# Latent attention loop: the pieces of the next heads made 512 queries at a time, their second set exchanged by four transfers

## The reference, cut to what matters

```
c_q = h @ w_down_q.T
c_kv = h @ w_down_kv.T
q = (c_q @ w_up_q.T).reshape(b, s, H, DH).transpose(0, 2, 1, 3)
k = (c_kv @ w_up_k.T).reshape(b, s, H, DH).transpose(0, 2, 1, 3)
q = _apply_rope_subspace(q, DR)
k = _apply_rope_subspace(k, DR)
...
rot = jnp.stack([e * cos - o * sin, e * sin + o * cos], axis=-1)
...
attn = jax.nn.softmax(scores, axis=-1)
out = jnp.einsum('bhqk,bhkd->bhqd', attn, v)
```

## Time and profile before

| | |
|---|---|
| median of 3 runs | 2046.2 us (2045.5 to 2050.0) |
| profiled execution, own time | 2044.6 us |
| its span in the trace | 2042.6 us |
| PE busy | 1862.5 us (91%) |
| DVE busy | 1593.6 us (78%) |
| ACT busy | 1270.9 us (62%) |
| POOL busy | 1066.7 us (52%) |
| loop of the latent attention | from about 640 to about 1900 us of the span |

### The profile page before, as it was taken

The page is one execution under the profiler, slowest core; times in us unless marked ns, Lnnn a source line. Parts: engine busy times, 40 slices in busy tenths (PEclk is TensorE's granted clock), DMA queues, the critical chain, the costliest instruction groups (busy, mean ns, idle before and its releaser), DMA issues. The chain is left out here.

```text
span 2042.6 us, 36152 instructions
## 1 busy us (share of the span) xinstructions
PE 1862.5 (91%) x11446; PEld 930.9 (46%) x11446; DVE 1593.6 (78%) x2433; ACT 1270.9 (62%) x2613; POOL 1066.7 (52%) x1218
## 2 busy tenths in 40 slices
PE   5764898989868999999999999999999999999798
PEld 2552476547643444444444443444443444444446
DVE  6786866686656888887888887888888888888455
ACT  6432685368625777776777776777777677777331
POOL 0644842583215656655665664665665566566200
PEclk9997999999988999999999999999999999999799
DMA  1001122012044998998889999898998889999353
GB/s 38 1 1 69 38 46 74 6 36 47 15 156 169 343 330 322 345 327 314 321 323 333 336 329 327 301 342 323 336 337 324 313 326 329 341 326 335 128 115 73
DMA packets 201614, 454.27 MB, mean 222 GB/s; under 512 B 12065, under 2 KB 159265, under 8 KB 200257
## 3 DMA queue, kind: packets, MB, share of 16 engines
q1 hardware_dynamic: 201408, 451.76, 62.8%
HBM read 230.86 MB, written 206.83 MB: 214 GB/s over the span
## 5 line engine op out<-in xcount | busy, mean ns | idle before, releaser
L1637 ACT ACTIVATE g.probs<-g_score,g.lowest 128x1024 f32<-128x1024 f32 x514 | 568.0, 1109 | 335.4 <-DVE g.lowest L1623 331.2
L1623 DVE TENSOR_REDUCE g.lowest<-g_score 128x1 f32<-128x1024 f32 x514 | 605.5, 1219 | 185.6 <-PE g_score L1591 185.6
L1591 PE MATMUL g_score<-g.keys,g.queries 64*128 64x512 f32 x2056 | 502.3, 607 | 20.0 <-issue 11.0
L1733 DVE STREAM_TRANSPOSE g.blocks<-g.probs 128x768 f32<-128x768 f32 x512 | 467.0, 950 | 2.4 <-ACT g.probs L1637 1.5
L1653 PE MATMUL g_mix_ps<-g.far,mid.y_tok 128*64 128x512 f32 x1560 | 377.7, 605 | 0.0
L1591 PEld LDWEIGHTS g_score<-g.keys,g.queries 64*128 64x128 f32 x2056 | 183.9, 188 | 250.2 <-ACT g.probs L1637 131.5
L1693 POOL TENSOR_TENSOR g.scaled<-g.scaled,g.coef 128x1024 f32<-128x1024 f32 x66 | 125.1, 1896 | 237.9 <-ACT g.scaled L1685 230.1
L1753 POOL TENSOR_TENSOR mid.y_tok<-mid.y_tok,g.waves 128x512 f32<-128x512 f32 x128 | 162.3, 1268 | 72.8 <-ACT mid.y_tok L1606 72.8
L1613 PEld LDWEIGHTS g_turned<-top.ident,g.probs 128*128 128x128 f32 x1024 | 107.8, 141 | 195.5 <-issue 194.8
L1380 POOL TENSOR_TENSOR g.queries<-mid.y_tok 64x256 f32<-64x256 f32 x256 | 185.4, 724 | 19.6
L1613 PE MATMUL g_turned<-top.ident,g.probs 128*128 128x128 f32 x1024 | 168.8, 288 | 0.0
(11 more groups left out here) (370 smaller groups left out, 2757.4 us busy)
## 6 DMA issues: line engine op xcount, KB each, us to landing
g.far<-bounce SPq DMA_DIRECT2D x257, 768.0 KB, 7.0
bounce<-g.blocks SPq DMA_DIRECT2D x256, 768.0 KB, 6.0
e.share<-shares SPq DMA_DIRECT2D x8, 1024.0 KB, 17.8
g.far<-g.near SPq DMA_DIRECT2D x7, 768.0 KB, 12.3
lt.early<-turns SPq DMA_DIRECT2D x2, 2048.0 KB, 9.2
lt.early<-la0.v SPq DMA_DIRECT2D x6, 512.0 KB, 9.2
lt.early<-la1.v SPq DMA_DIRECT2D x6, 512.0 KB, 8.8
bounce<-g.near SPq DMA_DIRECT2D x4, 768.0 KB, 15.3
```

What stands on the lines that cost most here:

```text
L1591: nc.tensor.matmul(score[:, 2 * pair + odd], queries[rows, turn, head, cols], keys[rows, turn, head, pair * CH:(pair + 1) * CH], start=Tru ...
L1623: nc.vector.tensor_reduce(lowest[:, unit, half, r:r + 1], score[:, 2 * half:2 * half + 2].rearrange("p b n -> p (b n)"), AX.X, ALU.max, ne ...
L1637: nc.scalar.activation(probs[:, r % 2, half * 2 * CH:(half + 1) * 2 * CH], score[:, 2 * half:2 * half + 2].rearrange("p b n -> p (b n)"), ...
L1733: ins = nc.vector.transpose(blocks[:, r, :, REST * half:REST * (half + 1)].rearrange("p j t c -> p t j c"), probs[:, r % 2, at:at + REST * ...
```

## The change

PE makes pieces once in a body, in step 1: 512 positions, and only the set with the rows in order (2 matmuls of 512 columns in place of 8 instructions' worth of 256 columns twice). ACT copies them once, in step 2. SP then issues four transfers that copy `raw` to a new buffer `exchanged` with neighbouring groups of 32 partitions swapped. POOL multiplies the four sets of 512 (`turn_pieces`) and adds them (`place_pieces`), all behind the second `add_output` of the body and ahead of `totals(this)`. The semaphore counts follow.

```diff
-            for swap in range(2):
-                for kind in range(2):
-                    ins = projected(side[:, kind, swap * QH:(swap + 1) * QH], turn, kind, swap,
-                                    slice(at * QH, (at + 1) * QH))
+            for kind in range(2):
+                ins = projected(side[:, kind], turn, kind, 0, slice(at * CH, (at + 1) * CH))
             ins.then_inc(m["piece_full"], 1)
...
+        def exchange(sync, n):
+            sync.wait_ge(m["piece_taken"], n + 1)
+            for k in range(4):
+                sync.dma_start(exchanged[32 * k:32 * k + 32], raw[32 * (k ^ 1):32 * (k ^ 1) + 32])\
+                    .then_inc(m["exchanged"], 16)
+
+        def turn_pieces(pool, at, n):
+            pool.wait_ge(m["exchanged"], 64 * (n + 1))
+            for swap in range(2):
+                for kind in range(2):
+                    part = (raw, exchanged)[swap][:, kind].rearrange("p (a n) -> p a n", a=2)
+                    nc.gpsimd.tensor_tensor(part, part, waves[:, 2 * at:2 * at + 2, swap], ALU.mult)\
+                        .then_inc(m["order"], 1)
+
+        def place_pieces(pool, turn, at, n, kind):
+            first, second = raw[:, kind], exchanged[:, kind]
             if kind == 0:
                 for head in range(2):
-                    place_keys(nc.gpsimd, turn, head, at, QH, first, second).then_inc(m["order"], 1)
-                    pool.wait_ge(m["order"], n + 2 + head)
+                    pool.wait_ge(m["order"], 10 * n + 4 + head)
+                    place_keys(nc.gpsimd, turn, head, at, CH, first, second).then_inc(m["order"], 1)
+                pool.wait_ge(m["order"], 10 * n + 6)
             else:
                 for crossed in range(2):
                     for head in range(2):
-                        place_queries(nc.gpsimd, turn, head, head ^ crossed, at, QH, first, second)\
+                        place_queries(nc.gpsimd, turn, head, head ^ crossed, at, CH, first, second)\
                             .then_inc(m["order"], 1)
-                    pool.wait_ge(m["order"], n + 3 + 2 * crossed)
-            pool.sem_inc(m["parts_ready"], 1)
+                    pool.wait_ge(m["order"], 10 * n + 8 + 2 * crossed)
+                pool.sem_inc(m["parts_ready"], 1)
...
                                 write_blocks(sync, w, 2, G + 2)
+                                if w == 0:
+                                    exchange(sync, 4 * g + j)
                                 read_blocks(sync, w, 1, G + 1)
...
                             add_output(pool, (2 * j + 1) % 4, (j + 2) % NC, H)
-                            make_parts(pool, 1 - turn, 2 * j, H, 0)
+                            n = 4 * g + j
                             totals(pool, last, H - 1)
-                            make_parts(pool, 1 - turn, 2 * j, H, 1)
-                            make_parts(pool, 1 - turn, 2 * j + 1, H + 1, 0)
                             coefs(pool, last, H - 1)
                             gaps(pool, this, H)
-                            make_parts(pool, 1 - turn, 2 * j + 1, H + 1, 1)
                             add_output(pool, (2 * j + 2) % 4, (j + 3) % NC, H + 1)
+                            turn_pieces(pool, j, n)
+                            place_pieces(pool, 1 - turn, j, n, 0)
+                            place_pieces(pool, 1 - turn, j, n, 1)
                             totals(pool, this, H)
                             coefs(pool, this, H)
...
-                                        pieces(pe, 1 - turn, 2 * j)
-                                    elif step == 3:
-                                        pe.wait_ge(m["piece_taken"], H + 1)
-                                        pieces(pe, 1 - turn, 2 * j + 1)
+                                        pieces(pe, 1 - turn, j)
...
-                                        take_pieces(act, H)
+                                        take_pieces(act, 4 * g + j)
                                         falls(act, H - 1)
...
-                                    elif step == 4:
-                                        take_pieces(act, H + 1)
```

More of the change, by code:

```diff
@@ L1347, in latent_attention @@
         scaled = sp.sb("scaled", [P, 2, RT * D])
+        exchanged = sp.sb("exchanged", [P, 2, CH])
         bounce = nc.dram_tensor("bounce", (2 * RT, P * 4 * RUN), F32).ap()
@@ L1360, in latent_attention @@
               "gap_ready", "fall_ready", "weighted_ready", "total_ready", "inverse_ready", "combined", "mixer_loaded0",
-              "mixer_loaded1", "mixers_stored", "tail_landed")}
+              "mixer_loaded1", "mixers_stored", "tail_landed", "exchanged")}
         mixer_loaded = [m["mixer_loaded0"], m["mixer_loaded1"]]
@@ L1595, in pieces, with take_pieces @@
         def pieces(pe, turn, at):
-            for swap in range(2):
-                for kind in range(2):
-                    ins = projected(side[:, kind, swap * QH:(swap + 1) * QH], turn, kind, swap,
-                                    slice(at * QH, (at + 1) * QH))
+            for kind in range(2):
+                ins = projected(side[:, kind], turn, kind, 0, slice(at * CH, (at + 1) * CH))
             ins.then_inc(m["piece_full"], 1)
-        def take_pieces(act, half):
-            act.wait_ge(m["parts_ready"], 2 * half + 2)
-            act.wait_ge(m["piece_full"], half + 1)
+        def take_pieces(act, n):
+            act.wait_ge(m["parts_ready"], n + 1)
+            act.wait_ge(m["piece_full"], n + 1)
             nc.scalar.activation(raw[:], side[:], ACT.Copy).then_inc(m["piece_taken"], 1)
@@ L1789, in _ @@
                                 if j == 0 and w == 0:
-                                    sync.wait_ge(m["piece_full"], H + 1)
+                                    sync.wait_ge(m["piece_full"], 4 * g + 1)
                                     load_w(sync, turn, g + 2)
                                 write_blocks(sync, w, 2, G + 2)
+                                if w == 0:
+                                    exchange(sync, 4 * g + j)
                                 read_blocks(sync, w, 1, G + 1)
@@ L1804, in _ @@
                 pool.sem_inc(m["added"], 1)
-                pool.sem_inc(m["parts_ready"], 2)
+                pool.sem_inc(m["parts_ready"], 1)
                 pool.sem_inc(m["combined"], 3)
@@ L1850, in _ @@
                                             on = 1 - turn
-                                            pe.wait_ge(m["parts_ready"], 16 * (g + 1) + 2)
+                                            pe.wait_ge(m["parts_ready"], 4 * (g + 1) + 1)
                                     step = 4 * w + r
@@ L1872, in _ @@
                                         pe.wait_ge(w_loaded[1 - turn], 16 * (i + 1 + turn))
-                                        pieces(pe, 1 - turn, 2 * j)
-                                    elif step == 3:
-                                        pe.wait_ge(m["piece_taken"], H + 1)
-                                        pieces(pe, 1 - turn, 2 * j + 1)
+                                        pieces(pe, 1 - turn, j)
                                     elif step == 4:
-                                        pe.wait_ge(m["piece_taken"], H + 2)
+                                        pe.wait_ge(m["piece_taken"], 4 * g + j + 1)
                                         pe.wait_ge(m["mixed_ready"], U + 1)
```

## The result

The changed kernel takes 2297.2 us (median of 4 runs, 2294.9 to 2303.2) where the kernel before takes 2046.4 us beside it: ratio 1.1226, 95% interval 1.1201 to 1.1252. The profiled execution took 2294.9 us, its span is 2293.1; the one before had 2042.6, so 250.5 us were added. Forecast was 2326 us.

A forecast was written before the change was run, and what follows sets the result against it. PE was taken to set the pace. Bodies of 46.10 us, 50.76 with j = 3, mean 47.27 against 38.49, times 32 add 281 us to 2044.6, giving 2326 us; range 2250 to 2370.

The forecast's parts named there:

- The bound and the step that decides: Step 7: DVE's inverse waits about 7.8 us for POOL's totals, queued behind ten piece instructions, in three bodies of four.
- t: Moment when ACT takes a body's second output; step 7's inverse was forecast at t + 19.70, not t + 11.90.
- the row of 1.70: Profile row of a 64x512 POOL addition taking 1.70 us, ascribed to DVE multiplying two SBUF tiles; the sum used 1.26.
- j = 3: Every fourth body: PE itself waits for parts_ready ahead of step 7's scores, idle about 11 us; body 50.76 us.
- The clock: PE's clock falls to its low level behind each coming gap, at a price of 2.36 us per fall.
- rival A: The clock holds behind PE's gaps: body 44.07 us, 48.40 with j = 3, total 2258 us; chance 0.16.
- the 2.36 of the rows: Price of a clock fall on PE from profile rows: 1.80 us scores to transposes plus 0.56 to the output.
- The body: Loop body: 46.10 us with j = 0, 1, 2 and 50.76 with j = 3, mean 47.27 against 38.49.
- 281: Forecast added time in us for the whole loop: 8.78 us more per body, times 32 bodies.
- What lies outside the loop, and the three jumps back, stays.: Time outside the loop's bodies and at its three jumps back was taken as unchanged, adding nothing to the sum.
- The exchange at no cost: SP's transfers of 0.5 MB a body stay hidden at 7 to 10 us, deciding only if over 14 us.
- Rival C: POOL's totals come in time for step 7's inverse, leaving only step 3's 0.87 us saving: 2017 us; chance 0.03.

The follow-up runs named there:

- experiment 1: The changed kernel with POOL's totals(this) moved ahead of its ten instructions on the pieces: 2107.7 us, 1.0304 of the kernel before.
- experiment 6: The changed kernel with PE computing step 0's output seven times where j > 0, as filler in the gap: 2247.0 us, ratio 1.0986.
- experiment 3: experiment 2 without the exchange transfers, the second set made from rows in order, so the partner swap is left out: 2017.5 us, ratio 0.9865.
- experiment 5: experiment 2 with the exchange issued sooner, ahead of SP's wait for mix_done and the read behind it: 2038.6 us, ratio 0.9962.
- experiment 2: The changed kernel with the exchange one transfer earlier and POOL's ten piece instructions and totals(this) before the second add_output: 2082.0 us, ratio 1.0180.

## Why the prediction was right, and where it was off

**The bound and the step that decides.** Right, and shown by experiment 1: DVE's inverse in step 7 waits for totals that POOL makes 7.4 us too late (7.8 forecast; 184.6 us of waits in all, against some 185). The sizes: inverse at t + 19.36 for t + 19.70, since the multiplications follow one another without the 0.08 us that I had taken from dependent instructions (2.50 for two, not 2.70). The additions measured 1262 to 1264 ns each, the value that I had chosen; scores 4.49 after the inverse, as forecast. PE's gap was 5.52 us where I had over 6, and the DMA share 0.81 where I had under 0.8.

My reading of the row of 1.70 named the wrong instruction of DVE. Its multiplication (L1566) reads one tile from SBUF and one, `score`, from PSUM, and POOL's addition beside it takes 1.27 us. What stands beside the long one is DVE's own addition of two tiles from SBUF (L1375), in the kernel before:

```profile
623.80 0.69 DVE L1375 TENSOR_TENSOR g.keys<-g.probs 64x512 f32<-64x512 f32 x1
...
623.93 1.69 POOL L1375 TENSOR_TENSOR g.keys<-g.probs 64x512 f32<-64x512 f32 x1
...
627.66 2.48 DVE L1566 TENSOR_TENSOR g.probs<-g_score,g.waves 128x512 f32<-128x512 f32 x4 [3.17 <-PE g_score L1369]
...
628.38 1.27 POOL L1375 TENSOR_TENSOR g.keys<-g.probs 64x512 f32<-64x512 f32 x1
```

The choice of 1.26 us isn't touched by it: DVE's loop has no such addition.

**j = 3.** Right: PE waits 10.3 us for `parts_ready` (about 11 forecast), and the body without a jump takes 50.7 us for 50.76.

**The clock.** Right, in kind and in size. The low clock stood behind each of the 24 gaps of 5.5 us (3.4 to 3.7 us from scores to transposes) and behind the waits with j = 3. In the forecast the body with the fall and the body of rival A lie 46.10 - 44.07 = 2.03 us apart, less than the 2.36 of the rows, since without the fall the second half of the scores waits for an exponential; experiment 6 gives 2.1. By the Trainium skill (TensorE: Matmul & The Clock Gate, section HAM oscillation) waits between bursts bring the slow clock back each time; the changed kernel agrees, with 24 gaps of 24 and a mean clock of 0.90 from 1000 to 1200 us. Rival A, 2258 us, falls.

**The body.** Over four bodies without a jump, j = 3 to j = 3, the inverses of step 7 lie 187.65 us apart in DVE's timeline:

```profile
1203.35 0.17 DVE L1719 RECIPROCAL g.inverse<-g.total 128x4 f32<-128x4 f32 x1
...
1391.00 0.17 DVE L1719 RECIPROCAL g.inverse<-g.total 128x4 f32<-128x4 f32 x1
```

That is 46.91 each for 47.27. The 0.36 us, times 32, are 11.5 of the 30 us between 281 and 250.5. They lie in the bodies with j = 0, 1, 2, which take 45.6, 45.1 and 46.3 us for 46.10 (from one inverse of step 4 to the next), most of it the 0.34 us by which the inverse of step 7 comes earlier.

**The term that failed: "What lies outside the loop, and the three jumps back, stays."** The sum put the cost of the jumps in the changed kernel at what it was before, without a row for it, and it was all but gone. Before, the bodies behind them took 5.1, 6.3 and 4.6 us longer (inverses of steps 7 and 4 lie 29.63, 30.83 and 29.12 us apart there, 24.49 elsewhere), 16.1 us together. After, four bodies with a jump take only 0.1 to 0.2 us longer than four without: 1015.53 to 1203.35 is 187.82, 1203.35 to 1391.00 187.65, 827.80 to 1015.53 187.73. 11.5 and 16.1 are 27.6 of the 30 us; the rest, under 3 us, is left unexplained. That 2326 came within 29 us of 2297.2 is not luck: the mechanism is the one forecast, and both misses made the forecast too high, so they did not cancel.

**The exchange at no cost.** Right for the change, at 46.9 us a body and a DMA share of 0.81: POOL never waited for it. But I priced its load only at the slow body's length. At 37.6 us a body the same sum gives 0.92 x 1.04 x 38.49 / 37.62 = 0.98, and there it costs 21 us by load alone and, issued late, 43 more by waiting. Rival C's 2017 us is what experiment 3 takes without the exchange; with it, 2038.6 is the best that was found. In the orders that were tried, three quarters of the 28 us that PE gains are lost again to the exchange, by the load or by waits for it.

## What to carry to other kernels

Ask of each block of work that is moved on an in-order engine which small result stands behind it, and who waits for that result at which fixed place: here 13 us on an engine that is half idle, moved ahead of two instructions of 0.2 us, cost 190 us. A saving on the busiest engine shortens the loop and with it the time in which the transfers must fit; sum their share at the new length before they are made to replace matmuls. And a gap on PE can cost more than its length, here 1.2 to 2.7 us more.

## What the runs showed of the hardware that was not expected

- Gaps of 1.94 to 1.98 us behind 4.7 us of small matmuls (64x128) had the low clock behind them in 16 of 24 places (scores of up to 3.68 us) and not in the other 8 (2.22), with the same instructions ahead of them; 0.18 us behind 6.5 us of such matmuls left 2.23. The length of the gap alone doesn't decide. What does, and whether the small matmuls matter, wasn't tried.
- The loss of about 5 us at a jump back of the loop is all but gone where PE waited in front of it: the changed kernel and experiment 1, with waits of over 10 us for `parts_ready` at the end of the pair, show no stall of PE that waits for nothing in the profile, while experiment 3, without that wait, shows 3, 11.8 us together, where the kernel before has 3, 11.0 us together. In between, experiment 5 waits 0.9 to 2.8 us ahead of the jumps and has stalls of 2.1 to 2.7 us, and experiment 2 waits 5.0 to 5.5 us and has one of 1.3 us behind one of its three jumps. Why wasn't tried.
- Four transfers of 128 KB keep SP's queue for 2.4 to 4.7 us to issue (2.4 to 3.3 in experiment 2, 3.9 to 4.7 in the changed kernel), where one of 768 KB takes 0.32 us to write and 0.37 to read, by the median; in the changed kernel SP has that time.
